# ViT attention stage on one NeuronCore: softmax normalised an image at a time, three images in the ring, y read by VectorE

## The reference

```python
qkv = fake_quant(x) @ fake_quant(ww1).T
dots = einsum('bhnd,bhmd->bhnm', fake_quant(q), fake_quant(k)) * scale
a = softmax(dots)
out = einsum('bhnm,bhmd->bhnd', fake_quant(a), fake_quant(v))
h = h + fake_quant(out) @ fake_quant(ww2).T + bb2
```

## Time and profile before

| | us |
|---|---|
| median of 3 runs (1443.85 to 1445.03) | 1444.19 |
| the profiled execution | 1445.15 |
| its span | 1443.2 |
| TensorE, VectorE, ScalarE, GpSimd busy | 1218.4, 1209.8, 990.7, 457.1 |

### The profile page before, as it was taken

How to read it: one execution, slowest core, us unless ns; L and a number is a source line. 1 busy time by engine, 2 the same in 40 slices (tenths; PEclk the granted TensorE clock), 3 DMA queues, 4 the chain that set the end, 5 groups by cost and what they waited for, 6 DMA issues and landing times.

```text
span 1443.2 us, 40676 instructions
## 1 busy us (share of the span) xinstructions
PE 1218.4 (84%) x11806; PEld 761.2 (53%) x11806; DVE 1209.8 (84%) x2868; ACT 990.7 (69%) x2005; POOL 457.1 (32%) x540
## 2 busy tenths in 40 slices
PE   5999992999999999999999999999846766767676
PEld 5999991445555555555555555555523333333343
DVE  4566782269999999999999999999978999999996
ACT  0000002568888888888888888888817888888886
POOL 7344541001111111111111111111126666666664
PEclk9999995569999999999999999999956787777765
DMA  6999972124444444444444444444532222222222
GB/s 246 267 281 276 299 246 64 44 76 117 119 120 120 120 120 120 120 120 120 120 119 121 120 119 119 117 120 117 126 75 61 83 82 82 82 82 86 83 73 69
DMA packets 142650, 182.38 MB, mean 126 GB/s; under 512 B 40528, under 2 KB 104784, under 8 KB 142288
## 3 DMA queue, kind: packets, MB, share of 16 engines
q1 hardware_dynamic: 71472, 134.72, 31.7%
q10 hardware_dynamic: 55776, 37.45, 8.8%
q0 software_dynamic: 15360, 9.70, 5.7%
HBM read 147.31 MB, written 34.50 MB: 126 GB/s over the span
## 4 chain that ended last, share of the span: by engine, by line
PE 74%; DVE 9%; issue 7%; ACT 5%; ACTq 2%; DMA 1%; DVEq 0%; SPq 0%; POOL 0%
PE psum L1044 13%; PE psum L1161 13%; PE psum L1101 12%; PE psum L1149 8%; PE psum L1108 7%; PE psum L1183 5%; PE psum L1126 5%; PE psum L1118 4%; PE psum L1120 2%; DVE big L1002 2%; ACT xT L500 2%; PE psum L1093 1%; PE psum L1204 1%; DVE oo L1019 1%; ACT big L574 1%
## 5 line engine op out<-in xcount | busy, mean ns | idle before, releaser
L913 DVE TENSOR_TENSOR pi<-big 128x788 int16<-128x788 f32 (+1 forms) x384 | 370.4, 965 | 0.0
L677 POOL DMA_DIRECT2D h_res<-att x128 | 118.1, 959 | 724.1 <-ACT att L520 722.4
L544 ACT ACTIVATE big<-psum 128x788 f32<-128x788 f32 (+1 forms) x384 | 314.8, 820 | 2.9 <-DVE pi L913 2.9
L1101 PE MATMUL psum<-xT,w1b 96*128 96x197 bf16 x1536 | 196.3, 259 | 43.3 <-ACT xT L500 43.3
L504 ACT ACTIVATE qki<-psum 128x394 int16<-128x394 f32 x384 | 179.1, 498 | 59.2 <-PE psum L1101 54.7
L1161 PE MATMUL psum<-big,sa_hot 128*32 128x197 f32 (+1 forms) x3072 | 216.0, 355 | 0.0
L1044 PE MATMUL psum<-big 128*128 128x192 f32 (+1 forms) x1200 | 197.3, 330 | 19.3 <-DMA big<-xt 17.3
L1044 PEld LDWEIGHTS psum<-big 128*128 128x128 f32 (+1 forms) x1200 | 195.4, 190 | 20.3 <-DVE big L722 17.2
L766 DVE TENSOR_SCALAR pT<-pi,lo,hi 128x788 bf16<-128x788 int16 (+1 forms) x384 | 185.3, 483 | 22.3
L1101 PEld LDWEIGHTS psum<-xT,w1b 96*128 96x128 bf16 x1536 | 124.6, 100 | 124.9 <-issue 65.8
L1183 PE MATMUL psum<-winb,zT 96*128 96x512 bf16 (+1 forms) x396 | 150.3, 548 | 34.8 <-DVE big L1002 34.2
(11 more groups left out here) (105 smaller groups left out, 1966.1 us busy)
## 6 DMA issues: line engine op xcount, KB each, us to landing
big<-z_row SPq DMA_DIRECT2D x192, 394.0 KB, 3.8
big<-xt SPq DMA_DIRECT2D x98, 384.0 KB, 4.3
tin<-h_res SPq DMA_DIRECT2D x49, 192.0 KB, 2.4
tres<-h_res ACTq DMA_DIRECT2D x49, 192.0 KB, 2.5
out<-oo ACTq DMA_DIRECT2D x49, 192.0 KB, 2.6
h_res<-hp ACTq DMA_DIRECT2D x96, 96.0 KB, 3.8
h_res<-att POOLq DMA_DIRECT2D x64, 96.0 KB, 3.5
x_int<-xb ACTq DMA_DIRECT2D x96, 48.0 KB, 3.9
```

The costliest lines, as they stand in the source:

```text
L544: act.activation(ex[0:r, U1 * par + u, :, :].rearrange("p (a h) n -> p a h n", a=2), psum[0:r, 2 * (u % 2):2 * (u % 2) + 2, 0:2 * N] .rear ...
L913: v.tensor_tensor(pi[0:r, t, :, 0:N], ex[0:r, w % U1 + U1 * ((par + w // U1) % 2), :, :], zb[0:r, g, :, :], ALU.mult).then_inc(s_pi, 1)
L1101: last = mm(psum[:, bank, j * N:(j + 1) * N], w1b[:, c, ch:ch + 128], xT[:, c, :], start=(c == 0), stop=(c == 1))
```

## The change

The unit of VectorE's work in the softmax becomes an image's whole token tile, 12 heads x 197 elements: two products and two clips an image in place of six and six. The exponentials are kept in a ring of three images (`ex`, indexed by `tri` = b mod 3), so is the clipped v (`vb`); `zb`, `pT` hold two images. The memory for that comes from laying tiles of the first stage into the same region. PV of an image is now wholly in step b + 3, as the first entries of slots 1 to 3, and waits for both clips of its image; inside a piece the two halves of the partitions alternate, for each token tile in turn. y moves to the end of slot 5, and VectorE reads it in the next step (L898 of the changed kernel) in place of ScalarE. The steps go to b = 67, and the loop has 9 rounds of six steps. The arithmetic of every element is the same.

```diff
--- before.py
+++ after.py
@@
-        SLOTS = [[("v", 3, 0), ("o", 2, -3), ("xt", 0, 1)],
-                 [("qk", 0, 1), ("qk", 1, 1)],
-                 [("o", 0, -2), ("qk", 2, 1), ("v", 0, 1)],
-                 [("qk", 3, 1), ("qk", 4, 1), ("qk", 5, 1)],
-                 [("o", 1, -2), ("y", 0, -3)],
-                 [("y", 1, -3), ("v", 1, 1), ("v", 2, 1)]]
+        SLOTS = [[("v", 3, 0), ("xt", 0, 1)],
+                 [("o", 0, -3), ("qk", 0, 1), ("qk", 1, 1)],
+                 [("o", 1, -3), ("qk", 2, 1), ("qk", 3, 1)],
+                 [("o", 2, -3), ("qk", 4, 1), ("qk", 5, 1)],
+                 [("v", 0, 1), ("v", 1, 1)],
+                 [("v", 2, 1), ("y", 0, -3), ("y", 1, -3)]]
...
@@ over_images
-            with eng.Fori(0, (B - 8) // 2) as i:
-                step(2 * i + 5, 1)
-                step(2 * i + 6, 0)
-            for b in range(B - 3, B + 3):
-                step(b, b % 2)
+                step(b, b % 2, b % 3)
+            rounds = (B - 8) // 6
+            with eng.Fori(0, rounds) as i:
+                for j in range(6):
+                    step(6 * i + 5 + j, (5 + j) % 2, (5 + j) % 3)
+            for b in range(5 + 6 * rounds, B + 4):
+                step(b, b % 2, b % 3)
@@ sync
                     wait_apart(sp, s_zinv, b)
+                    wait_apart(sp, s_zb, 48 * (b - 1))
                     for g in range(3):
-                        wait_apart(sp, s_zb[g], 16 * (b - 1))
-                        sp.dma_start(z_row[g, :, :], zinv[g:128:32, 0:N]).then_inc(s_zrow[g], 16)
-                if has_unit(b, -U1):
+                        sp.dma_start(z_row[g, :, :], zinv[g:128:32, 0:N]).then_inc(s_zrow, 16)
+                    wait_apart(sp, s_zrow, 48 * b)
+                    wait_apart(sp, s_pi, 2 * b - 4)
                     for g in range(3):
-                        wait_apart(sp, s_zrow[g], 16 * b)
-                        wait_apart(sp, s_pi, 6 * (b - 2) + 2 * g + 2)
-                        sp.dma_start(zb[:, g, :, :].rearrange("p h n -> p (h n)"),
+                        sp.dma_start(zb[:, 1 - par, 4 * g:4 * g + 4, :].rearrange("p h n -> p (h n)"),
@@ scalar: read_piece, image_step
-                elif kind == "y":
-                    r = TOK[k][1]
-                    ip = par if d % 2 == 0 else 1 - par
-                    if not isinstance(im, int) or im > 1:
-                        wait(act, s_added[ip], added(im, ip))
-                    act.activation(att[0:r, ip, k, :], psum[0:r, bank, 0:D], ACT.Copy,
-                                   scale=factor[F_Y]).then_inc(evac[kind], 1)
...
-                        wait(act, s_pi, U - 11)
+                        wait(act, s_pi, 2 * b - 5 + t)
@@ gpsimd
-                if has_unit(b, -3 * U1):
+                if has_unit(b, -4 * U1):
...
+                        wait_apart(pool, evac["y"], 2 * b - 7 + t)
@@ vector (the step before is in the listing above; this one replaces it)
+                def clip_probs(image, ip, t):
+                    r = TOK[t][1]
+                    dve.wait_ge(s_pi, 2 * image + t + 1)
+                    wait(dve, full["o"], 3 * (image - 1))
+                    clip(pT[0:r, ip, t, :, 0:N], pi[0:r, t, :, 0:N], None, r, ZA).then_inc(s_pb, 1)
+
+                def normalise(image, ip, it, t):
+                    r = TOK[t][1]
+                    dve.wait_ge(s_zb, 48 * (image + 1))
+                    dve.wait_ge(s_exp, U1 * (image + 1))
+                    wait(dve, s_pb, 2 * image + t - 1)
+                    v.tensor_tensor(pi[0:r, t, :, 0:N], ex[0:r, it, t, :, :], zb[0:r, ip, :, :],
+                                    ALU.mult).then_inc(s_pi, 1)
+
+                def clip_qk(half):
+                    dve.wait_ge(evac["qk"], 6 * (b + 1) + 3 * (half + 1))
...
+                if has_unit(b, -U1):
+                    dve.wait_ge(evac["v"], 4 * b)
+                    wait(dve, full["o"], 3 * (b - 3))
+                    clip(vb[:, (tri + 2) % 3, :, :], vi[:, nxt, :, :], None, 128, ZV).then_inc(s_vb, 1)
+                if has_unit(b, -4 * U1):
+                    for t, (_, r) in enumerate(TOK):
+                        dve.wait_ge(full["y"], 2 * b - 7 + t)
+                        if t == 0 and (not isinstance(b, int) or b > 5):
+                            wait(dve, s_added[par], added(b - 4, par))
+                        v.tensor_scalar(att[0:r, par, t, :], psum[0:r, bank_of(NP - 2 + t), 0:D],
+                                        fac[0:r, F_Y:F_Y + 1], None, ALU.mult).then_inc(evac["y"], 1)
+                if has_unit(b, -3 * U1):
+                    clip_probs(b - 3, nxt, 1)
+                if has_unit(b, -U1):
...
+                if has_unit(b, -2 * U1):
+                    normalise(b - 2, par, (tri + 1) % 3, 0)
+                if exists(b, 1):
+                    clip_qk(0)
+                if has_unit(b, -2 * U1):
+                    clip_probs(b - 2, par, 0)
+                if exists(b, 1):
+                    clip_qk(1)
+                if has_unit(b, -3 * U1):
+                    dve.wait_ge(evac["o"], 3 * b - 6)
+                    wait(dve, full["y"], 2 * b - 6)
+                    clip(ob[:, :, 0:N], oi[:, nxt, :, :], None, 128, ZX2).then_inc(s_ob, 1)
+                if has_unit(b, -2 * U1):
+                    normalise(b - 2, par, (tri + 1) % 3, 1)
@@ tensor: product, image_step
-                    G = 3 * im + k
-                    pe.wait_ge(s_pb, 2 * G + 2)
+                    it = (tri + d) % 3
+                    pe.wait_ge(s_pb, 2 * im + 2)
                     pe.wait_ge(s_vb, im + 1)
-                    for i in range(4):
-                        head, j, po = 4 * k + i, ORD.index(i), (i % 2) * DH
-                        dst = psum[po:po + DH, bank, (i // 2) * N:(i // 2 + 1) * N]
-                        mm(dst, vb[:, ip, 0, head * DH:(head + 1) * DH], pT[:, k, 0, j, 0:N],
-                           start=True, stop=False)
-                        last = mm(dst, vb[0:R1, ip, 1, head * DH:(head + 1) * DH], pT[0:R1, k, 1, j, 0:N],
-                                  start=False, stop=True)
+                    for c in range(2):
+                        for t, r in ((0, 128), (1, R1)):
+                            for i in range(2):
+                                head, j = 4 * k + 2 * c + i, 4 * k + ORD.index(2 * c + i)
+                                last = mm(psum[i * DH:(i + 1) * DH, bank, c * N:(c + 1) * N],
+                                          vb[0:r, it, t, head * DH:(head + 1) * DH], pT[0:r, ip, t, j, 0:N],
+                                          start=(t == 0), stop=(t == 1))
```

More of the change, by code:

```diff
@@ L163, in vit_tower_kernel @@
         s_zinv = sem("softmax_inverse_ready")
-        s_zb = [sem(f"softmax_inverse_spread_{g}") for g in range(3)]
-        s_zrow = [sem(f"softmax_inverse_stored_{g}") for g in range(3)]
+        s_zb = sem("softmax_inverse_spread")
+        s_zrow = sem("softmax_inverse_stored")
         s_pi = sem("probs_int16_ready")
@@ L483, in _ @@
                 act.dma_start(dram[:, 0, :], src[0:B, 0, 2, :]).then_inc(s_st1[0], 16)
-            def added(image, par):
-                return 32 * ((image - par) // 2) if isinstance(image, int) else 16 * (image - par)
             def read_piece(b, par, n):
                 kind, k, d = PIECES[n]
-                if not exists(b, d) or (isinstance(b, int) and b + d < 0):
+                if kind == "y" or not exists(b, d) or (isinstance(b, int) and b + d < 0):
                     return
@@ L533, in _, with image_step @@
                 act.reg_load(factor[k], fac[0:1, k:k + 1].bitcast(i32))
-            def image_step(b, par):
+            def image_step(b, par, tri):
                 n = 0
@@ new lines, in clip_qk @@
+                def clip_qk(half):
+                    dve.wait_ge(evac["qk"], 6 * (b + 1) + 3 * (half + 1))
+                    wait(dve, s_scores, 6 * b)
+                    clip(qkb[:, nxt, 6 * half:6 * half + 6, 0:N], qki[:, 6 * half:6 * half + 6, :], None,
+                         128, (ZQ, ZK)[half]).then_inc(s_qkb, 1)
+                if has_unit(b, -U1):
+                    dve.wait_ge(evac["v"], 4 * b)
+                    wait(dve, full["o"], 3 * (b - 3))
+                    clip(vb[:, (tri + 2) % 3, :, :], vi[:, nxt, :, :], None, 128, ZV).then_inc(s_vb, 1)
@@ new lines, in image_step @@
+                if has_unit(b, -3 * U1):
+                    clip_probs(b - 3, nxt, 1)
+                if has_unit(b, -U1):
+                    dve.wait_ge(s_zsum, b)
+                    wait(dve, s_zti, b - 1)
+                    v.transpose(zt[:, :, :].rearrange("p a b -> p (a b)"), psum[:, 4, 0:NZ]).then_inc(s_zt, 1)
+                    dve.wait_ge(s_zt, b)
+                    wait(dve, s_zinv, b - 1)
+                    v.reciprocal(zti[:, :, 0:3], zt[:, :, 0:3]).then_inc(s_zti, 1)
+                    dve.wait_ge(s_zti, b)
+                    wait(dve, s_zrow, 48 * (b - 1))
```

(7 more changed lines are left out.)

104 lines of the change are left out of this document (32 added, 72 removed).

## The result

| | before | after |
|---|---|---|
| median, us | 1444.02 | 1602.91 |
| lowest and highest of 4 runs | 1443.13 to 1445.03 | 1574.28 to 1609.94 |
| the profiled execution | 1445.15 | 1574.28 |
| its span | 1443.2 | 1572.5 |

The account below looks back on a forecast made before the run. TensorE was taken to set the pace at 12.14 us an image; the new loop over VectorE would make it 12.36, so 58 steps give +12.8, less 0.5 for fewer loop rounds: +12, 1456 us, range 1430 to 1497.

Parts of the forecast that it names:

- the loop over VectorE: Attention stage, from one o0 to the next: VectorE's chain and TensorE's slots sum to 12.36 us an image against 12.14.
- the loop over images: Hardware loop of the attention stage: 9 rounds instead of 28, at most some hundredths each, -0.5 us in all.
- the chain of VectorE: Part of the 12.36 us sum, from the second qk clip to the end of the probabilities' clip: 5.46 us.
- handoff: From VectorE's clip to the o piece on TensorE: 0.11 us, upper end 0.24.
- the y reads: VectorE's two reads of y out of PSUM, in its chain: 0.27 us of issue each.
- VectorE's instructions: Softmax on VectorE: the merged multiplication takes 2.61 us, the merged clip 0.88.
- the rival of the merging that does not save: Long VectorE instructions as dear as three short ones: 13.2 us an image, 1505 us; part of the upper range, no separate chance.
- TensorE's waits: Wait for xT goes; TensorE waits for VectorE before xt and before o0, 0.9 us an image together.
- VectorE's: VectorE's waits: idle some 2 us an image ahead of the second qk clip.
- Alternating halves: Matmul order inside PV's pieces: the halves already overlap, so worth 0, lower end -0.3 us.
- The clock: Rival: waits around xt drop TensorE to 1.2 GHz, 6.8 us more per such image; chance 0.16.
- one image of ten: Clock rival's milder case: one image in ten at 1.2 GHz, +39 us, 1495 us.

Follow-up runs that it names:

- e13: Changed kernel with only TensorE keeping the loop of six steps, all other engines' programs over the images written out: 1585.11 us, 1.092.
- e14: Changed kernel with TensorE's and ScalarE's programs over the images written out, the other engines keeping the loop of six steps: 1486.11 us, 1.027.
- e9: Changed kernel with only TensorE's program over the images written out, the other engines keeping the loop of six steps: 1538.49 us, 1.061.
- e5: Changed kernel with its loop over images written out on all engines: 1483.64 us, 1.028.
- e10: Kernel before with 14 rounds of four steps in its loop over images: 1444.64 us, 1.000.
- e7: Kernel before with 9 rounds of six steps in its loop over images in place of 28 of two: 1544.60 us, 1.068.
- e11: Changed kernel with y read by ScalarE, v clipped late and no loop over images, but PV's matmuls in the old order: 1410.61 us.
- e6: Changed kernel with y read by ScalarE, v clipped late and the loop over images written out: 1409.28 us, 0.975.
- e8: Changed kernel with six extra TensorE multiplications ahead of o0 and the loop over images written out: 1464.20 us, 1.013.
- e12: Kernel before with ScalarE copying xT twice, which lengthens TensorE's wait: 1625.47 us, 1.125.

## Why the prediction was wrong

The profiled executions are 129 us apart (1445.15 and 1574.28). The transposes of the sums in 58 images of the stage tell where:

| in the changed kernel's trace | us |
|---|---|
| the loop over VectorE: 58 images, 12.47 for 12.14 | +19 |
| the jumps: the two images at each of eight, 8.2 to 10.5 more than two of 12.47 | +75 |
| six images with a fall of the clock between the jumps, 4.6 to 6.1 more than 12.47 | +33 |

The executions of 1596 us and more have no trace, so what they have beyond this isn't shown. The engines' parts don't add up: TensorE's jumps alone cost 1585 - 1486 = 99 us (e13 against e14, with the falls that came along), ScalarE's alone 52 (e9 against e14). In the changed kernel, where both jump, TensorE waited for ScalarE's late exponential three times only, 3.6 us together.

- **The step that failed is the one on the loop over images: "The loop over images has 9 rounds instead of 28; it costs at most some hundredths each, -0.5 in all."** I counted rounds and did not ask how long the body gets. A short body's jump does cost hundredths (0.05 us with two and with four steps), but with six steps TensorE stands still for 3.2 us in this kernel and 4.4 in the old order, and the clock falls behind it. That is 75 of the 129 us between the profiled executions; without any loop the median falls by 119 (e5). The Trainium skill states the rule that I had passed over ("Runtime: NRT & Kernel Launch", Instruction fetch mechanics): a jump whose target has left the engine's instruction memory must fetch it before anything executes. The packets of q8 agree with it. It gives TensorE 2048 instructions. A step has 3327 x 12.14/280 = 144 matmuls and as many weight loads, so four steps are 1152 of them and six 1728; with the register, branch and semaphore instructions the traces have some 1270 and 1900 (e10, e7). The edge that the runs show lies between the two, and both are below 2048, so that figure doesn't give it. The same section also speaks of a window of two pages, which by its 256 instructions a page is 512; by that two steps would stop as well, and they don't. For ScalarE, to which it gives 512, it does not tell the kernels apart: the stops of 4 to 7 us showed in kernels where ScalarE doesn't read y (some 280 instructions in six steps), none where it does (some 310).
- **The loop over VectorE: right in mechanism, 0.11 short.** Forecast 12.36 us, measured 12.47. From `o0` to the second qk clip 712.53 - 705.78 = 6.75 (forecast 4.08 + 2.71 = 6.79), the chain of VectorE 5.66 (5.46), handoff 0.06 (0.11). What was too small is vb, 0.59 for 0.49, and the y reads, 0.65 for 0.54 together. Taking y out gives 0.66 back and confirms the chain; moving vb gives 0.35 of its 0.59, so close behind the chain stands another bound.
- **VectorE's instructions: right.** 2.60 and 0.90 for 2.61 and 0.88; the rival of the merging that does not save is out.
- **TensorE's waits: right; VectorE's: half.** The wait for xT is gone; ahead of `xt` 0.6 and ahead of `o0` 0.4, 1.0 together for 0.9. VectorE waits 1.0 us ahead of the second qk clip, for the 2 forecast, and 0.7 ahead of the first.
- **Alternating halves: right**, 0, and the Trainium skill's rule of order ("TensorE: Matmul & The Clock Gate", Part 3) would have given 0.3 us an image, which no run shows: with and without the alternation it is 11.60 us (e11, e6).
- **The clock: the rival was named, its size was not.** The price of a fall, 6.8 us, was near (18.57 - 12.50 = 6.1 in e5). The waits alone made three falls in 58 images in e5, six in the changed kernel's trace and seven in e14, +18 to +33 us: about the rival's "one image of ten". What the rival lacked is the stop at the jump, behind which the clock fell each of eight times.
- Without the jumps the time lies within 1430 to 1497, at 1484 us (e5), but 38 us above the kernel before and not 12: some 20 for the loop over VectorE, 18 for three falls.

Left open: why ScalarE's program is fetched again in some kernels and not in others, what made one execution of e8 take 1856 us, why the number of falls differs between executions with the same waits, and whether a body of five steps would do (the ring of three and the pairs need a multiple of six, so it wasn't tried).

## What to carry to other kernels

When a change lengthens the body of a hardware loop, because a ring gets another period, count the instructions of each engine's body, and look in the trace for a stop without a releaser at the first instruction of a round, and for instruction packets in the middle of the loop. Writing the loop out was worth 119 us here by the medians, and the order's merit could only be seen after that: with y on ScalarE and v's clip out of the chain it is some 37 us faster than before. A wait of TensorE has two prices, its length and the clock that it may cost; where the bound is TensorE, a few matmuls of no use in the wait can be cheaper than the wait (1464 for 1484 us), though they were no surety: one execution of four took 1856.

## What the runs showed of the hardware

- A jump back over six steps stops TensorE for 3.0 (e13) to 4.4 us (e7), over four or two steps it costs 0.05. It is TensorE's own: it stays when all others have no loop (e13). ScalarE's goes when ScalarE's program is written out as well (e14).
- Bodies of two and four steps are jumped back over without a fetch; the body of six is fetched in every round (no q8 packet against 62 and 63 between 400 and 1000 us).
- Waits of TensorE once an image: 0.67 us, no fall in 58 images; 0.56, none in the profiled execution of e8; 0.56 and 0.46 apart by 0.4 us of work, three in one trace (e5) and seven in another (e14); 1.20 in one, 25 (e12). In e12 half a microsecond of waiting an image cost 30 us by itself and some 150 by the clock.
- In the image behind a fall TensorE is busy without a gap, at 0.50, and yet the clock stays there for 17 us. Windows of the changed kernel from 340 us on:

```profile
341.00:345.00 4.00, 4.00 (x33) 2.38 (x32) 1.57 (x1) 2.31 (x5) 0.00 (x0) 0.50 0.29 70
345.00:350.00 5.00, 5.00 (x41) 2.46 (x42) 1.92 (x4) 3.44 (x7) 0.00 (x0) 0.50 0.56 216
```

- The Trainium skill ("TensorE: Matmul & The Clock Gate", Part 1) lets the clock fall after the engine was idle. The stops at the jump agree with it; the falls behind waits of 0.56 and 0.46 us, or of one of 1.20, with work between and around them, do not. They are closer to what the same part calls a second failure mode, where short idle times between groups of matmuls make the clock go down and up.
